# Attention's last tile and the start of the feed-forward part in a two-layer adaLN kernel: the tile reordered without its state sums, weight rounding on three engines, feed-forward's first group turned and rounded inside attention

## The chip, the cores and the metric

One core of one Trainium2 chip runs the whole computation in one launch. The metric is the device time of that launch in microseconds, as the median of several runs. The engines are TensorE (PE; its weight loads are PEld), VectorE (DVE), ScalarE (ACT), GpSimd (POOL) and SyncE (SP), which issues the transfers.

## The reference, cut to what matters

Two transformer layers over x of (2, 1024, 256), each an attention-like part and a feed-forward part, each behind a layer norm whose scale and shift come from a conditioning vector. Layer 0's attention is linear attention: 16 heads, 4 key/value heads, features elu(rope(q)) + 1, and a state that runs over the sequence. Its feed-forward part follows directly.

```python
h = _layernorm(x) * (1 + ca) + sa
# attention, per head, over the positions in order:
state = state + k_s[..., :, None] * v_s[..., None, :]
z = z + k_s
num = einsum('bhe,bhed->bhd', q_s, state)
den = einsum('bhe,bhe->bh', q_s, z)[..., None] + EPS
out = num / den
x = x + ga * (out @ Wo.T)
# feed-forward
h = _layernorm(x) * (1 + cb) + sb
h2 = silu(h @ w_gate) * (h @ w_up)
x = x + gb * (sparsify_2to4(h2) @ w_down)     # the two largest magnitudes of each four stay
```

Layer 1 (a test-time-training scan, then a mixture of experts) comes after that and is not touched but for where two of its buffers lie.

## The kernel before

The kernel is one program of four phases, each a block of its own with one instruction stream for each engine, ordered by hand with semaphores: attention_phase, ffn_phase, scan_phase, moe_phase. Between two blocks all engines meet. x stays in SBUF (x_sb) for the whole kernel, as 16 tiles of 128 positions, 8 for each of the two batches.

Attention walks the tiles as (c, b): c = 0 to 7 is the position in the sequence, b the batch, so the last two are (7, 0) and (7, 1). A tile is computed in chunks: within it the masked scores, before it the state. In step(c, b) TensorE turns the features of this tile (k, then four groups of q), computes for each of the four key/value heads the scores (L727), the numerators from masked scores and from the state (L735, L736), turns the normalised result (out_turn, L717), and at the end the sum k x v of this tile for the state (L774) and the output product with Wo (L786). Between these it projects q, k, v of the next tile (p(j), L689). VectorE masks the scores (masked, L575), normalises (L584, L587, L589), applies rope to the next tile's projections (L514, L517; GpSimd adds the two parts, L396), finishes the features (L529), adds the tile's sum to the state (L646), and adds the gated output to x (L658, L662). ScalarE drains what is turned (L419) and takes the exponentials. num is one PSUM buffer: numerators(g + 1) wait until normalise(g) has read numerators(g). score_masked and score have two slots.

Matrices that need more than fp32r's precision are split into a high part, rounded to fp32r, and a low part, the rest rounded: a product is three passes, high x high, low x high, high x low. For weights this is split_chunk, in chunks of 512 columns: chunk_high (L132 on VectorE, L130 on ScalarE) and chunk_low (L139). The four chunks of the feed-forward's gate and up weights go over the columns of the attention weights in w_hi and w_lo, so they can be written when the last projection, that of tile (7, 1) done during (7, 0), is through. Three of them are in the staging buffer a_stage early; the fourth reuses the first one's slot, and its transfer waits until the first has been rounded. In the last tile, which has no next tile to project, VectorE does all four splits between its masks and normalisations:

```python
for i in range(2 * FI // WCH):
    self.split_chunk(dve, NW + i, i * WCH)
    if i == 0:
        masked(1)
    if i == 1:
        normalise(1)
```

The feed-forward works on 4 groups of 4 tiles (512 positions). Of group 0 (tiles 0 to 3 of batch 0, long finished), VectorE takes the statistics (ffn_norms, L207, L210) and, after GpSimd's rstd (L214, L216), centres it into g_xn (ffn_centre, L223) at the end of the last attention tile. The rest of group 0 is in ffn_phase, behind the meeting of the engines: TensorE turns it (norm_turn, L1106), ScalarE applies scale and shift (drain_norm, L936), VectorE rounds it (split, L981, L983), and TensorE starts on hidden(0, 0), that is, gate and up product of 128 of the 1024 hidden columns, six matmuls of 512 columns each (L1117). m counts the 8 such blocks. In front of split(0) VectorE's queue has the statistics of group 1, behind it its centring; TensorE turns group 1 behind block m = 1.

## Time and profile before

| what | us |
|---|---|
| median of 3 runs | 1032.14 (1031.8 to 1033.04) |
| the profiled execution: time | 1031.37 |
| its span | 1029.6 |
| PE busy | 976.8 (95%) |
| DVE busy | 681.7 (66%) |
| ACT busy | 332.3 (32%) |
| POOL busy | 249.5 (24%) |
| mean granted clock of TensorE | 0.995 |

The profile is one execution. Times within it count from the start of its span. Attention takes the first 543 us, the feed-forward part of layer 0 follows. In a timeline each row is one instruction or a merged run of them: start, duration, engine, line of the kernel, operation, what it writes and reads, how often, and in brackets how long the engine was idle before it and what ended that. A duration includes the time an instruction spends in the pipeline, so the distance between starts tells what one costs its engine. The granted clock is 1.00 for 2.4 GHz and 0.50 for 1.2 GHz.

### The profile page before, as it was taken

Reading aid. Unit: us, or ns where it says so; the run is one execution under the profiler, and the core shown is the slowest. Engines: PE = TensorE matmul, PEld = TensorE weight load, DVE = VectorE, ACT = ScalarE, POOL = GpSimd, SP = SyncE. Lnnn points to the kernel's source line nnn. Section 1 sums busy time; section 2 is a strip of 40 time slices with the busy share of each in tenths; the row PEclk is TensorE's granted clock in tenths of the full one; section 3 lists DMA queues with packets and bytes.
Section 4 is the critical chain, followed back from the end, with each engine's and each line's share of the span. In section 5 each row is a group of like instructions: output and inputs, shape, how many; then the busy total and the mean of one; then the engine's idle time right before and its main releaser. Section 6 shows DMA issues by size and latency. Waiting matters only on the chain. (4 is left out here: it accounts for less than half of the span.)

```text
span 1029.6 us, 15693 instructions
## 1 busy us (share of the span) xinstructions
PE 976.8 (95%) x5994; PEld 791.1 (77%) x5994; DVE 681.7 (66%) x1494; ACT 332.3 (32%) x604; POOL 249.5 (24%) x320
## 2 busy tenths in 40 slices
PE   5899999999999999999978999998999999999997
PEld 4688888888888888888856788885666667778875
DVE  6766766666766667666565977765676776476556
ACT  4343333433333343334313323221122232422220
POOL 2232312222212323122201010023334554211011
PEclk9999999999999999999998999999999999999999
DMA  9400000000000000000004000002455340000000
GB/s 297 142 1 1 1 1 1 1 1 1 1 1 1 1 1 2 1 1 1 1 21 137 1 1 1 1 1 42 124 115 113 92 84 22 1 16 16 11 21 20
DMA packets 33051, 33.37 MB, mean 32 GB/s; under 512 B 6857, under 2 KB 26834, under 8 KB 32978
## 3 DMA queue, kind: packets, MB, share of 16 engines
q1 hardware_dynamic: 32978, 32.38, 11.9%
q8 instruction: 48, 0.79, 0.3%
q14 instruction: 25, 0.20, 0.1%
HBM read 23.98 MB, written 8.13 MB: 31 GB/s over the span
## 5 line engine op out<-in xcount | busy, mean ns | idle before, releaser
L396 POOL TENSOR_TENSOR rope_sum<-rope_cos,rope_sin 128x512 f32<-128x512 f32 x80 | 115.0, 1437 | 257.0 <-DVE rope_sin L517 257.0
L432 ACT ACTIVATE rope_exp<-rope_sum 128x512 f32<-128x512 f32 x80 | 50.5, 631 | 205.2 <-POOL rope_sum L396 205.1
L786 PE MATMUL proj<-wo_sb,attn_out_t 128*128 128x256 f32 x512 | 113.2, 379 | 0.7 <-issue 0.7
L786 PEld LDWEIGHTS proj<-wo_sb,attn_out_t 128*128 128x128 f32 x512 | 96.1, 190 | 13.4 <-issue 0.9
L735 PE MATMUL num<-v_ones,score_masked 128*128 128x129 f32 x512 | 99.2, 275 | 5.9 <-DVE score_masked L575 5.9
L736 PE MATMUL num<-state,q_t 128*128 128x129 f32 x512 | 99.0, 275 | 0.0
L2052 DVE SCALAR_TENSOR_TENSOR m_acc<-m_expert,gates,m_acc 128x256 f32<-128x256 f32 x128 | 61.9, 484 | 46.3 <-PE m_expert L2101 39.9
L735 PEld LDWEIGHTS num<-v_ones,score_masked 128*128 128x128 f32 x512 | 82.1, 191 | 13.4 <-DVE score_masked L575 8.0
L514 DVE TENSOR_TENSOR rope_cos<-proj,cos_sb 128x512 f32<-128x512 f32 x80 | 55.3, 691 | 52.3 <-PE proj L689 52.3
L689 PE MATMUL proj<-w_hi,a_h_hi 128*128 128x512 f32 x192 | 79.0, 493 | 4.1 <-DVE w_lo L139 2.4
L736 PEld LDWEIGHTS num<-state,q_t 128*128 128x128 f32 x512 | 77.7, 192 | 0.0
L529 DVE SCALAR_TENSOR_TENSOR feat<-rope_sum,rope_exp 128x512 f32<-128x512 f32 x80 | 69.1, 863 | 7.0 <-ACT rope_exp L434 7.0
L727 PE MATMUL score<-q_t,k_t 128*128 128x512 f32 x128 | 66.9, 605 | 0.0
L2101 PE MATMUL m_expert<-w_sb,m_act 128*128 128x256 f32 x256 | 62.9, 385 | 2.9 <-DVE m_acc L2052 2.9
L717 PEld LDWEIGHTS turn<-ident,feat 128*128 128x128 f32 x320 | 38.3, 143 | 32.3 <-issue 25.8
L1519 DVE TENSOR_TENSOR t_w<-g_ps,head_blocks 128x512 f32<-128x512 f32 x64 | 44.2, 691 | 27.9 <-PE g_ps L1727 27.9
L1128 PE MATMUL f_rows<-wd_sb,hidden 128*128 128x256 f32 x256 | 58.1, 380 | 3.3 <-DVE hidden L1021 1.5
L689 PE MATMUL proj<-w_lo,a_h_hi 128*128 128x512 f32 x192 | 60.9, 398 | 0.0
L689 PE MATMUL proj<-w_hi,a_h_lo 128*128 128x512 f32 x192 | 60.9, 398 | 0.0
L2101 PEld LDWEIGHTS m_expert<-w_sb,m_act 128*128 128x128 f32 x256 | 47.3, 190 | 14.5 <-DVE m_acc L2052 8.5
L1128 PEld LDWEIGHTS f_rows<-wd_sb,hidden 128*128 128x128 f32 x256 | 48.1, 190 | 11.8 <-issue 4.3
L717 PE MATMUL turn<-ident,feat 128*128 128x128 f32 x320 | 46.6, 277 | 9.8 <-ACT k_t L419 9.8
(250 smaller groups left out, 1883.6 us busy)
## 6 DMA issues: line engine op xcount, KB each, us to landing
kv_scratch<-t_kv SPq DMA_DIRECT2D x16, 256.0 KB, 2.4
kv_rows<-kv_scratch SPq DMA_DIRECT2D x32, 128.0 KB, 3.7
a_stage<-in_wqkv SPq DMA_DIRECT2D x6, 512.0 KB, 5.3
wo_sb<-in_wo SPq DMA_DIRECT2D x1, 2048.0 KB, 9.6
a_stage<-in_wgu SPq DMA_DIRECT2D x4, 512.0 KB, 9.7
out<-x_sb SPq DMA_DIRECT2D x16, 128.0 KB, 1.7
u_scratch<-u_rows SPq DMA_DIRECT2D x28, 64.0 KB, 2.9
t_u<-u_scratch SPq DMA_DIRECT2D x14, 128.0 KB, 2.2
```

The source lines that it names most:

```text
L396: pool.tensor_tensor(y[:, parity], t1[:, parity], t2[:, parity], ALU.add).then_inc(s["y_done"], 1)
L514: dve.tensor_tensor(t1[:, parity].rearrange("p (g d) -> p g d", d=HD // 2), proj[:, bank, :].rearrange("p (g d) -> p g d", d=HD // 2), cc. ...
L529: dve.scalar_tensor_tensor(dst, y[:, parity], 0.0, ex[:, parity], ALU.max, ALU.add).then_inc(s["feat_done"], 1)
L689: mm = pe.matmul(proj[:, bank, :], hh[:, parity, k, :], ww[:, k, cols], start=(i == 0 and k == 0), stop=(i == 2 and k == KD - 1))
L717: t = pe.transpose(turn[:, bank(j), r * P:(r + 1) * P], src[:, r * P:(r + 1) * P], ident[:])
L727: pe.matmul(score[:, g % 2, :], k_t[:, g, :], q_t[:, g, :], start=True, stop=True).then_inc(s["score_full"], 1)
L735: pe.matmul(dst, am[:, g % 2, r * P:(r + 1) * P], v[:, b, g, :], start=True, stop=False)
L736: mm = pe.matmul(dst, q_t[:, g, r * P:(r + 1) * P], state[:, b, g, :], start=False, stop=True)
L786: mm = pe.matmul(proj[:, b, 0:D], o_t[:, i, :], wo[:, i, :], start=(i == 0), stop=(i == H - 1))
L1128: mm = pe.matmul(rows[:, n % 2, 0:D], hid[:, g % 2, m, i * P:(i + 1) * P], wd[:, m, :], start=(m == 0), stop=(m == NM - 1))
L2052: ins = dve.scalar_tensor_tensor(acc[:, n % 2], expert[:, k % 2, j * D:(j + 1) * D], gates[:, g % 2, i, e:e + 1], acc[:, n % 2], ALU.mult, ...
L2101: mm = pe.matmul(expert[:, k % 2, j * D:(j + 1) * D], act_t[g % 2][:, e, toks], w2[:, e, :], start=True, stop=True)
```

## The change

Five edits, all around tile (7, 0), tile (7, 1) and the start of the feed-forward part:

- The state sums of the last two tiles (eight matmuls L774 and the addition L646 each) are left out; nothing reads them. The count of num_full and num_free is shifted by one for tile (7, 1) (num_item).
- The rounding of the four chunks is spread: chunks 0 and 1 wholly on VectorE at the end of tile (7, 0), in front of the dx multiplication; the high parts of chunks 2 and 3 on ScalarE (at the end of (7, 0), and in (7, 1) behind the q drains), their low parts on GpSimd behind its last rope addition, in front of ffn_rstd(0).
- Tile (7, 1) has an order of its own on TensorE and on VectorE: the scores run up to two groups ahead of the numerators, and VectorE has masks, normalisations, and group 0's statistics and centring between them.
- Group 0 of the feed-forward is turned by TensorE in tile (7, 1), into the score buffer, in front of out_turn(3); ScalarE drains it behind the last attn_out_t drain, VectorE rounds it behind normalise(3). ffn_phase begins without its norm_turn(0), drain_norm(0) and split(0).
- For that, f_h and the first slot of f_h_hi and f_h_lo share their place with the attention's modulation weights (a_wmod) and, later, with m_h and m_h_hi of the last phase (one_place).

The diff, cut to its core:

```diff
@@ run
+        block = [P, KD, GT * P]
+        self.wmod0, = self.one_place(("a_wmod", [P, KD, 6 * D], F32))
+        self.f_in = self.one_place(("f_h", block, F32), ("f_h_hi0", block, F32R), ("f_h_lo0", block, F32R))
+        self.e_h, self.e_h_hi = sb("m_h", block), sb("m_h_hi", [P, 2, KD, GT * P], F32R)
...
@@ attention, shared
+            def num_item(c, b, j):
+                return at(c, b, KVH + 1, j) - (1 if last(c, b) else 0)
...
@@ attention, GpSimd
                 walk(pool, step)
+                for i in (2, 3):
+                    self.chunk_low(pool, NW + i, i * WCH)
                 ffn_rstd(pool, 0)
...
@@ attention, ScalarE
+                    if last(c, b):
+                        self.chunk_high(act, NW + 3, 3 * WCH)
                     for g in range(KVH):
                         drain_turn(c, b, 5 + g, o_t[:, g * REP:(g + 1) * REP, :],
...
                     e(3)
                     e(4)
+                    if (c, b) == (NC - 1, 0):
+                        self.chunk_high(act, NW + 2, 2 * WCH)
+                    if last(c, b):
+                        for k in range(KD):
+                            act.wait_ge(f_s["turn_full"], k + 1)
+                            act.activation(f_h[:, k, :], score[:, k, :], ACT.Identity,
+                                           bias=mod_t[:, 0, SB_ * KD + k, 0:1],
+                                           scale=mod_t[:, 0, CB * KD + k, 0:1]).then_inc(f_s["h_done"], 1)
...
@@ attention, VectorE
                     if last(c, b):
-                        for i in range(2 * FI // WCH):
-                            self.split_chunk(dve, NW + i, i * WCH)
...
+                        masked(0)
+                        masked(1)
+                        normalise(0)
+                        masked(2)
+                        ffn_norms(dve, 0)
+                        normalise(1)
+                        masked(3)
+                        normalise(2)
+                        ffn_centre(dve, 0)
+                        normalise(3)
+                        dve.wait_ge(f_s["h_done"], KD)
+                        dve.tensor_copy(f_hi[:], f_h[:]).then_inc(f_s["hi_done"], 1)
+                        dve.wait_ge(f_s["hi_done"], 1)
+                        dve.tensor_tensor(f_lo[:], f_h[:], f_hi[:].bitcast(F32), ALU.subtract).then_inc(f_s["hl_done"], 1)
...
+                        if c < NC - 1:
+                            dve.wait_ge(s["num_full"], num_item(c, b, KVH) + 1)
...
+                        q_rope(4)
+                        f(3)
+                        if c == NC - 1:
+                            for i in range(2):
+                                self.split_chunk(dve, NW + i, i * WCH)
...
@@ attention, TensorE
+                    if last(c, b):
+                        scores(1)
+                        q_turn(3)
+                        numerators(0)
+                        scores(2)
+                        numerators(1)
+                        out_turn(0)
+                        scores(3)
+                        numerators(2)
+                        out_turn(1)
+                        numerators(3)
+                        out_turn(2)
+                        pe.wait_ge(f_s["xn_done"], GT)
+                        pe.wait_ge(s["score_free"], 2 + at(c, b, KVH, KVH))
+                        for k in range(KD):
+                            for i in range(GT):
+                                t = pe.transpose(score[:, k, i * P:(i + 1) * P], self.g_xn[:, i, k * P:(k + 1) * P], ident[:])
+                            t.then_inc(f_s["turn_full"], 1)
+                        out_turn(3)
...
+                        if c < NC - 1:
+                            pe.wait_ge(s["num_free"], num_item(c, b, KVH) + 1)
+                            for g in range(KVH):
+                                mm = pe.matmul(num[:, g // 2, (g % 2) * VW:(g % 2 + 1) * VW],
...
@@ feed-forward
-                drain_norm(0)
...
-                split(0)
...
-                norm_turn(0)
```

## Rows read from the trace of the kernel before

**Rows 1.** Busy time by stretch: length, busy time of each engine, granted clock, DMA.

```profile
520.00:540.00 20.00, 15.37 (x96) 12.65 (x96) 12.66 (x29) 2.39 (x4) 1.23 (x2) 1.00 0.08 25
```

**Rows 2.** Timeline of TensorE in the last tile, (7, 1).

```profile
509.69 1.04 PE L717 MATMUL turn<-ident,feat 128*128 128x128 f32 x8
...
511.53 1.06 PE L727 MATMUL score<-q_t,k_t 128*128 128x512 f32 x2
512.43 0.60 PE L717 MATMUL turn<-ident,feat 128*128 128x128 f32 x4
513.45 0.49 PE L735 MATMUL num<-v_ones,score_masked 128*128 128x129 f32 x2 [0.42 <-DVE score_masked L575]
...
515.34 1.02 PE L727 MATMUL score<-q_t,k_t 128*128 128x512 f32 x2
...
519.15 0.49 PE L735 MATMUL num<-v_ones,score_masked 128*128 128x129 f32 x2 [2.36 <-DVE score_masked L575]
...
521.04 0.60 PE L717 MATMUL turn<-ident,attn_out 128*128 128x128 f32 x4
521.48 1.02 PE L727 MATMUL score<-q_t,k_t 128*128 128x512 f32 x2
...
533.23 0.60 PE L717 MATMUL turn<-ident,attn_out 128*128 128x128 f32 x4
534.57 7.14 PE L786 MATMUL proj<-wo_sb,attn_out_t 128*128 128x256 f32 x32 [0.73 <-issue]
```

**Rows 3.** Timeline of VectorE in the last tile.

```profile
515.54 0.16 DVE L584 TENSOR_SCALAR den<-num 128x4 f32<-128x4 f32 x1 [2.15 <-PE num L736]
...
515.95 0.69 DVE L589 TENSOR_TENSOR attn_out<-num,rden 128x512 f32<-128x512 f32 x1
516.55 0.68 DVE L132 CAST w_hi<-a_stage 128x1024 fp32r<-128x1024 f32 x1
...
518.41 0.68 DVE L575 TENSOR_TENSOR score_masked<-score,causal 128x512 f32<-128x512 f32 x1
...
534.05 1.39 DVE L207 BATCH_NORM_STATS2 g_stats<-x_sb 128x6 f32<-128x256 f32 x4
...
537.14 1.38 DVE L223 TENSOR_SCALAR g_xn<-x_sb,g_mv,g_rstd 128x256 f32<-128x256 f32 x4 [1.42 <-POOL g_rstd L216]
```

**Rows 4.** Timeline of TensorE at the start of the feed-forward part.

```profile
542.96 1.07 PE L1106 MATMUL f_turn<-ident,g_xn 128*128 128x128 f32 x8 [1.25 <-PEq L272]
547.12 1.22 PE L1117 MATMUL gate_ps<-f_h_hi,w_hi 128*128 128x512 f32 x2 [3.09 <-DVE f_h_lo L983]
...
552.14 0.63 PE L1117 MATMUL gate_ps<-f_h_hi,w_hi 128*128 128x512 f32 x2
...
554.89 1.03 PE L1106 MATMUL f_turn<-ident,g_xn 128*128 128x128 f32 x8
```

**Rows 5.** Busy time by stretch, columns as in rows 1.

```profile
545.00:551.50 6.50, 4.38 (x10) 3.47 (x11) 3.25 (x6) 1.96 (x3) 3.27 (x9) 0.50 1.04 396
```

**Rows 6.** Timeline of all engines at the end of tile (7, 0).

```profile
500.04 1.05 PE L774 MATMUL num<-v_ones,feat 128*128 128x129 f32 x8
...
500.87 1.29 ACT L419 ACTIVATE attn_out_t<-turn 128x512 f32<-128x512 f32 x2
...
502.78 0.59 PE L786 MATMUL proj<-wo_sb,attn_out_t 128*128 128x256 f32 x2
```

**Rows 7.** The same timeline, a little later.

```profile
504.35 1.27 POOL L396 TENSOR_TENSOR rope_sum<-rope_cos,rope_sin 128x512 f32<-128x512 f32 x1 [1.09 <-DVE rope_sin L517]
504.62 1.55 DVE L529 SCALAR_TENSOR_TENSOR feat<-rope_sum,rope_exp 128x512 f32<-128x512 f32 x1 [0.35 <-ACT rope_exp L434]
```

**Rows 8.** Line L139 on GpSimd: duration in ns (min/median/max), first and last start, forms.

```profile
L139 POOL TENSOR_TENSOR w_lo<-m_act,w_hi x3: 1263/2374/2375, 812.0 to 846.5; 128x1024 fp32r<-128x1024 f32 x2, 128x512 fp32r<-128x512 f32 x1
```

**Rows 9.** Tile a_stage: ScalarE's casts, columns as in rows 8, and the transfers' time to landing.

```profile
L130 ACT ACTIVATE w_hi<-a_stage x5: 1042/1060/1063, 11.9 to 24.0; 128x1024 fp32r<-128x1024 f32 x5
...
DMA to landing us min/median/max: 3.8/5.8/11.0
```

More of the change, by code:

```diff
@@ L107, in run, with one_place @@
         self.moe_phase()
+    def one_place(self, *tensors):
+        with ExitStack() as ctx:
+            return [ctx.enter_context(self.nc.sbuf_tensor(n, shape, dt)) for n, shape, dt in tensors]
     def stage_for(self, ctx, name, first, slots):
@@ L739, in out_turn @@
                     def out_turn(g):
[L740 removed]
+                        pe.wait_ge(s["num_free"], 2 + num_item(c, b, g))
                         turn4(5 + g, on[:, g % 2, :])
@@ L752, in step @@
                     q_turn(2)
-                    if nxt:
-                        pe.wait_ge(s["hl_done"], at(c, b, 1, 2))
-                    p(0)
-                    numerators(0)
-                    scores(1)
-                    q_turn(3)
-                    p(1)
-                    numerators(1)
-                    out_turn(0)
-                    scores(2)
-                    p(2)
-                    numerators(2)
-                    out_turn(1)
-                    scores(3)
-                    p(3)
@@ L1116, in hidden @@
                             for k in range(KD):
-                                mm = pe.matmul(dst[:, n % 2, :], ww[:, k, cols], hh[:, g % 2, k, :],
+                                mm = pe.matmul(dst[:, n % 2, :], ww[:, k, cols], hh[g % 2][:, k, :],
                                                start=(i == 0 and k == 0), stop=(i == 2 and k == KD - 1))
```

111 lines of the change are left out of this document (52 added, 59 removed).

## The prediction, made before the changed kernel ran

> **What bounds the kernel now.** I read three views in this order. The page shows a kernel bound by TensorE, which is busy nearly all the time; among the busy times by stretch, 520 to 540 us stands out with PE busy for only 15.4 of 20 us, at a granted clock of 1.00 [rows 1]. The timeline of TensorE in that place shows the last attention tile, from its first turn at 509.69 to the output product that begins at 534.57, with holes of 2.4 us in front of a group's numerators (two such; 519.15 is the first) [rows 2]. VectorE's timeline names what fills the holes: between two masks it rounds a chunk of the feed-forward weights (cast and subtraction, 1.86 us from 516.55 to the mask at 518.41; four chunks, one after the other, stand among the masks), so masked(1), which needs nothing but a score and a free VectorE, is 3 us late [rows 3]. Then the phase changes: after the last x add TensorE turns group 0 (542.96), and waits for ScalarE and for two roundings on VectorE until 547.12 [rows 4]. During that wait the granted clock falls to 0.50, that is 1.2 GHz, and stays there to 551.5 [rows 5]. So from 509 to 552 us the end is set by a handover between engines, and from there by TensorE again.
>
> **The change, part by part.** All times are of the profiled execution: span 1029.6, time 1031.37, so 1.77 us lie outside; the median of the runs, 1032.14, is 0.77 above it. I follow the path in its times.
>
> (a) Tile (7, 0) loses the eight matmuls of the state sum, 0.89 us from 500.04 to the next group, and VectorE an addition. Not all of the 0.89 is gained: the output product also needs the last attn_out_t drain, which ScalarE ends at 500.87 + 1.29 = 502.16 whatever TensorE does. With 0.1 from a drain to the product (an estimate; a handover from TensorE to VectorE takes 0.20, 515.34 to 515.54 [rows 2, 3]) it starts at 502.26 instead of 502.78: 0.52 gained [rows 6]. The last tile's first turn moves from 509.69 to 509.17.
>
> (b) Two chunks move to VectorE at the end of (7, 0), after its last feature (504.62 + 1.55 = 506.17 before; about 505.4 now, since the projection ahead comes some 0.8 earlier) [rows 7]. They take 2 x 1.86 and a few hundredths, to 509.3. The dx multiplication waits for the end of the output product, 509.2 now, plus 0.2: no later than without the chunks by more than some hundredths, and TensorE does not wait for it in the next tile. Free. ScalarE rounds the third chunk from 508.1 (it waits for VectorE's second cast) to 509.2, at 1.06 us [rows 9], ahead of the k_t drain that is due at 509.8. Free.
>
> (c) GpSimd subtracts chunk three from 509.3. On GpSimd such a subtraction took 2.37 us (two rows of 128x1024) [rows 8], so to 511.7. In that time VectorE has an x add and the last feature, both of two SBUF operands. The trace shows what that means: a feature begun at 504.62 took 1.55 us beside a GpSimd addition that ran from 504.35 for 1.27 [rows 7]; operations of this size alone take 0.68, like the mask in rows 3. It stood still until 505.62. So I put x add at 511.7, feature at 512.1 and masked(0) at 512.7 to 513.4. The new order lets numerators(0) start at 513.7 only (below), so 0.25 us is left over: cost 0. Bounds: 0 (a gain is excluded, the operation is an added one) and +2.1 (the subtraction takes twice as long); I take 0 because two rows give its length.
>
> The Trainium skill, page "SBUF — State Buffer", section "Who interferes with whom", says that a VectorE instruction with two SBUF inputs and a GpSimd instruction that reads SBUF exclude each other for the whole instruction. The trace agrees for a 1.27 us operation; no row shows it for one of 2.37. By the rule the sum stays; without any exclusion it would also stay, as the slack covers it.
>
> (d) The tile's new order. From the first turn to scores(0) is 1.84 us (509.69 to 511.53). Then scores(0), q_turn(2), scores(1), q_turn(3) at 0.90 (511.53 to 512.43), 0.45 (four turns, 521.04 to 521.48), 0.90, 0.45 [rows 2]: numerators(0) start at 509.17 + 1.84 + 2.70 = 513.71. From there a cycle decides: numerators take 1.89 (513.45 to 515.34), VectorE answers 0.20 later, normalise takes 1.10 (515.54 to 515.95 + 0.69), and some 0.06 later, the remainder of my reckoning, the next numerators may start [rows 2, 3]: 3.25 us a group, in which the score (0.90) and a turn (0.45) fit. One group is late: the four statistics and aggregates (from 534.05 to 537.14 - 1.42 = 535.72, 1.67 us) [rows 3] stand behind masked(2) and push normalise(1) by 0.12. So numerators start at 513.71, 516.96, 520.33, 523.58. After the last: 1.89, out_turn(2) 0.45, the eight turns of group 0 0.89 give 526.81, where on(3) is just ready: out_turn(3) at 526.85. From it to the output product 1.34 us, as before (533.23 to 534.57) [rows 2]. The product starts at 528.2 instead of 534.57, 6.4 earlier. The state matmuls that this tile loses (eight again, 0.89 us) and the 2.4 us holes are in that.
>
> (e) What must not be late for this. Chunk four is loaded when chunk one is done (507.4) and landed 3.8 to 11.0 us after its issue [rows 9]; ScalarE rounds it behind the q_t drains, 514.5 to 515.6, GpSimd subtracts to 518.0, and only then takes rstd of group 0, whose statistics come at 519.1. The centring (1.4 us) stands between normalise(2), done at 523.5, and normalise(3) at 525.7, where VectorE is free [rows 3]. Behind ScalarE's wait for the chunk only out_turn drains are queued. The chain may end 4 us later before it costs. Free.
>
> (f) Group 0's drain and rounding, for which TensorE sat idle 3.1 us ahead of 547.12 [rows 4], now lie beside the output product of 7.1 us [rows 2]. Cover: they start with the last drain, at 528.1, and would have to take over 8 us to show. So behind the phase change TensorE can begin with gate matmuls where it turned before. That removes 542.96 to 547.12, 4.16 us [rows 4]. VectorE is free for norms and centring of group 1: 1.67, 1.42 for rstd and 1.38, so done 4.5 us into the phase [rows 3], and norm_turn(1) stands behind two hidden blocks, 5.5 us in (twice the 2.75 of (g)). Free, with 1 us.
>
> (g) The clock. Before, the 12 gate and up pairs of groups m = 0 and 1 took 5.02 us (547.12 to 552.14, mostly at 0.50) and 2.75 (552.14 to 554.89, at full clock) [rows 4, 5]. If TensorE's only hole at the change of phase is the 1.3 us between product and first matmul, I take the full clock, since holes of 2.4 us in the tile left it at 1.00 [rows 1, 2]: 2.27 gained. Bounds: 0 (clock falls all the same) and 2.3.
>
> Sum: 6.4 (with 0.52 in it) + 4.16 + 2.27 = 12.8. Everything later hangs on TensorE and moves along unchanged. 1031.37 - 12.8 = 1018.6 for such an execution, span 1016.8; with 0.77, a median of 1019.3.
>
> **Rivals.**
> R1, the clock falls anyway. For it: the drain before the product and the barrier now stand 7 us apart, two holes near one another, and a long transfer starts there. Against it: before, the same two holes stood there, and the eight turns behind them took 1.07 us, no more than the eight at 509.69 with 1.04 [rows 2, 4]; the fall came in the wait of 3.1 us behind them. It costs 2.3: 1021.6.
> R2, the three-engine rounding comes back as a wait: GpSimd's subtraction holds x add and feature, or the rounding of chunk four is late for rstd. The first costs whatever exceeds 511.95, the second begins when the chunk's chain ends after 522.2, 4 us later than I put it. A chain 2 to 3 us worse than my figures gives 1021 to 1022.
> R3, the other side: chunk four's transfer. It is issued late and everything hangs on it in one line: ScalarE's cast, GpSimd's subtraction, rstd, centring, normalise(3), the product. Each us of landing beyond some 11 us after the issue delays the end by one. To be slower than before by 2 it must land 26 us after its issue, against 11.0 at most [rows 9]: 1034.5 (1019.3 + 15.2).
> R4, the holes close but the gain is not passed on: VectorE, the busiest engine after TensorE in the feed-forward part, becomes the limit of group 0. Its first product then moves less than TensorE. Against it: the page has TensorE busy nearly all the time there, so it does not wait for VectorE. I put the loss at no more than the 3 us of VectorE's norms and centring of group 1: 1022.3.
>
> **How the numbers follow.** The forecast has 0.66, R1 0.12, R2 0.11, R4 0.04, R3 0.02; 0.05 is left for a larger gain (a shorter phase change, as less is waiting in it: down to 1016.5). The forecast's own range is 1018 to 1020.5. To hold 8 in 10 I go to 1017.3 below and 1022.2 above. A measurement can tell about 0.2%, 2 us, from no change. Faster 0.96, same 0.02, slower 0.02.
>
> **What would show it.** Right: numerators of the last tile 3.2 to 3.4 us apart, an output product beginning near 528, no f_turn group before the first gate matmul at 536.5, granted clock 1.00 there and 2.75 us for m = 0. GpSimd's two w_lo rows at about 2.4 us, ending before 519. Wrong: a hole in front of q_turn(3) or numerators(0) released by VectorE, g_rstd late behind w_lo, a stretch at 0.50 after the barrier, or new waits of TensorE on hidden or silu_gate in group 0.

## The result and the profile after

The changed kernel took 1021.43 us (median of 13 runs, 1018.61 to 1032.28), the kernel before 1033.66 in as many runs beside it (1031.41 to 1035.42): a ratio of 0.9891, interval [0.9871, 0.9911], 12.2 us faster. The forecast was 1019.3 with a range of 1017.3 to 1022.2. The profiled execution took 1021.04 with a span of 1019.1; before it was 1031.37 and 1029.6.

| us | before | after |
|---|---|---|
| median of 13 runs each | 1033.66 | 1021.43 |
| span of the profiled execution | 1029.6 | 1019.1 |
| PE busy | 976.8 (95%) | 978.2 (96%) |
| DVE busy | 681.7 (66%) | 676.8 (66%) |
| ACT busy | 332.3 (32%) | 334.1 (33%) |
| POOL busy | 249.5 (24%) | 254.6 (25%) |
| second q turn of the kernel, the first with a long wait | 36.60 | 38.75 |
| output product of (7, 0) | 502.78 | 504.44 |
| output product of (7, 1) | 534.57 | 530.36 |
| first gate matmul | 547.12 | 538.75 |
| after the feed-forward part: next modulation vectors | 683.11 | 673.22 |
| first gradient of the scan | 710.99 | 701.09 |
| first expert product | 893.6 | 882.95 |

The stretch that opened the argument, busy time of each engine, granted clock and DMA, columns as in [rows 1]:

```profile
520.00:540.00 20.00, 17.17 (x107) 14.47 (x106) 10.28 (x29) 5.01 (x7) 1.30 (x3) 1.00 0.01 3
```

TensorE's timeline of the last tile and of the start of the feed-forward part, which answers to [rows 2, 4] (start, duration, instruction, idle before it and what ended that):

```profile
511.43 1.04 PE L744 MATMUL turn<-ident,feat 128*128 128x128 f32 x8
...
513.27 1.06 PE L754 MATMUL score<-q_t,k_t 128*128 128x512 f32 x2
...
515.90 0.39 PE L762 MATMUL num<-v_ones,score_masked 128*128 128x129 f32 x2
...
519.13 0.46 PE L762 MATMUL num<-v_ones,score_masked 128*128 128x129 f32 x2 [0.42 <-DVE attn_out L616]
...
522.44 0.46 PE L762 MATMUL num<-v_ones,score_masked 128*128 128x129 f32 x2
...
525.75 0.46 PE L762 MATMUL num<-v_ones,score_masked 128*128 128x129 f32 x2 [0.85 <-DVE attn_out L616]
...
528.05 1.04 PE L796 MATMUL score<-ident,g_xn 128*128 128x128 f32 x8
528.97 0.66 PE L744 MATMUL turn<-ident,attn_out 128*128 128x128 f32 x4
530.36 7.14 PE L832 MATMUL proj<-wo_sb,attn_out_t 128*128 128x256 f32 x32 [0.73 <-issue]
538.75 0.70 PE L1162 MATMUL gate_ps<-f_h_hi,w_hi 128*128 128x512 f32 x2 [1.25 <-PEq L281]
...
541.62 0.63 PE L1162 MATMUL gate_ps<-f_h_hi,w_hi 128*128 128x512 f32 x2
...
544.42 1.03 PE L1151 MATMUL f_turn<-ident,g_xn 128*128 128x128 f32 x8
```

The numerators follow each other every 3.23 to 3.31 us, where one step took 5.70 before (513.45 to 519.15). The holes of 2.4 us are gone; 0.42 and 0.85, both ended by a normalisation, are left. No turn stands between the meeting of the engines and the first gate matmul. Two blocks of m take 5.67 us (538.75 to 544.42) instead of 7.77, and the stretch that answers to [rows 5] stands at full clock:

```profile
538.70:545.00 6.30, 6.25 (x30) 5.15 (x31) 4.18 (x14) 3.12 (x4) 2.98 (x10) 1.00 0.79 281
```

GpSimd's timeline, its two subtractions:

```profile
511.42 2.36 POOL L148 TENSOR_TENSOR w_lo<-a_stage,w_hi 128x1024 fp32r<-128x1024 f32 x1 [4.29 <-ACT w_hi L139]
517.72 2.35 POOL L148 TENSOR_TENSOR w_lo<-a_stage,w_hi 128x1024 fp32r<-128x1024 f32 x1 [3.94 <-ACT w_hi L139]
```

VectorE's timeline, what it does beside the first of them, and group 0's rounding, which now lies beside the output product:

```profile
512.09 1.98 DVE L689 TENSOR_TENSOR x_sb<-x_sb,a_dx 128x256 f32<-128x256 f32 x1
513.99 0.68 DVE L556 SCALAR_TENSOR_TENSOR feat<-rope_sum,rope_exp 128x512 f32<-128x512 f32 x1
514.59 0.68 DVE L602 TENSOR_TENSOR score_masked<-score,causal 128x512 f32<-128x512 f32 x1
...
531.63 0.69 DVE L648 CAST f_h_hi<-f_h 128x1024 fp32r<-128x1024 f32 x1 [2.72 <-ACT f_h L496]
532.36 1.23 DVE L650 TENSOR_TENSOR f_h_lo<-f_h,f_h_hi 128x1024 fp32r<-128x1024 f32 x1
```

**Where the 10.5 us of the two spans come from**, as differences of the table's steps: the start of the kernel +2.15; from there to the product of (7, 0) -0.49; to the product of (7, 1) -5.87; to the first gate matmul -4.16; to the modulation vectors -1.52; to the scan's first gradient -0.01; the scan -0.75; the rest +0.15. The first step ends in the second q turn. The +2.15 lies 460 us ahead of the first edit, in a place whose instructions are the same. It is the spread of single executions, and the granted clock goes with it: between 26 and 28 us it was 1.00 in the profile of before and 0.50 in the one after (the last part of the next section shows the rows).

### The profile page after: what moved, and what is told of

It is laid out like the page before. It is cut to its first block and busy times, and to the rows that moved or that the text cites. A ratio compares the mean times of both kernels' runs of the same rounds, so it can differ in the third digit from the quotient of the medians.

```text
span 1019.1 us, 15660 instructions
## 1 busy us (share of the span) xinstructions
PE 978.2 (96%) x5978; PEld 790.9 (78%) x5978; DVE 676.8 (66%) x1488; ACT 334.1 (33%) x606; POOL 254.6 (25%) x322
## 5 line engine op out<-in xcount | busy, mean ns | idle before, releaser
L832 PEld LDWEIGHTS proj<-wo_sb,attn_out_t 128*128 128x128 f32 x512 | 96.0, 190 | 13.7 <-issue 1.3
```

The lines of the kernel that those rows point to most:

```text
L832: mm = pe.matmul(proj[:, b, 0:D], o_t[:, i, :], wo[:, i, :], start=(i == 0), stop=(i == H - 1))
```

## The experiments

All medians are of runs on the same chip as a kernel before; "product" is the output product of (7, 1), "gate" the first gate matmul, "mod" the modulation vectors behind the feed-forward part. The steps from one to the next are read in the profiles.

**e1 and e12: the changed kernel again**, with no edit, beside two groups of the others.

> The changed kernel once more. Theory A (the handover gained what the steps say, 12.8 us, and the rest of the distance is chance at the start of the kernel): the output product of the last tile begins 25.9 us behind the one of tile (7, 0) (504.44 to 530.36 in the first profile), the first gate matmul 8.4 us later, and where the first tile's first turn stands (36.6 before, 38.75 in the first profile) changes from run to run in both kernels; ratio 0.988. Theory B (the change itself makes the start slower): the first turn stands at 38.7 again and the kernel before has it at 36.6 each time; ratio 0.990.

> The changed kernel a third time, for the spread of its runs: 4 of 19 runs so far stood above 1025. Theory T (the change brings the far runs): some of six above 1025 again, more often than the kernel before stands 4 us above its median (3 of 47). Rival (they come to both kernels): none, or as many in both.

1020.48 (1019.04 to 1030.57, 6 runs; ratio 0.9884 [0.9846, 0.9921]) and 1021.62 (1019.51 to 1032.41, 6 runs; 0.9892 [0.985, 0.9934]). In each, five runs agree within 2.2 us and one lies 10 higher; such runs are called far runs from here on. In e1's profile the product came 25.91 us behind that of (7, 0) and the gate 8.40 later, as theory A has it; the second q turn stood at 38.73, which theory B expects too, and only e2 and e14 below part the two.

**e2: group 0's turn, drain and rounding back behind the meeting of the engines.**

```diff
@@ attention, TensorE, tile (7, 1)
-                        for k in range(KD):
-                            for i in range(GT):
-                                t = pe.transpose(score[:, k, i * P:(i + 1) * P], ...)
...
@@ feed-forward
+                drain_norm(0)
...
+                split(0)
...
+                norm_turn(0)
```

> The changed kernel with group 0's turn, drain and rounding back in the feed-forward phase; all else stays changed. Theory A: against the changed kernel 4.16 us for the serial steps come back and 2.27 for the clock, and the last tile is 0.9 shorter by the eight turns: together 5.5 us slower than it, with a stretch at 0.50 behind the wait. Rival (the clock term is wrong, it falls only by chance): 3.3 us slower, the granted clock in the first hidden blocks at 1.00.

1026.83 (1025.31 to 1032.88, 12 runs; 0.9945 [0.9927, 0.9963]), 6.35 above e1. TensorE's timeline, and the busy time by stretch:

```profile
536.65 1.06 PE L1137 MATMUL f_turn<-ident,g_xn 128*128 128x128 f32 x8 [1.25 <-PEq L281]
540.81 1.22 PE L1148 MATMUL gate_ps<-f_h_hi,w_hi 128*128 128x512 f32 x2 [3.09 <-DVE f_h_lo L1014]
```

```profile
539.00:545.80 6.80, 4.99 (x12) 3.93 (x13) 3.05 (x6) 1.66 (x2) 2.96 (x9) 0.51 1.03 390
```

The wait of 3.09 us is back, and with it the fall of the clock: product to gate takes 12.55 us again instead of 8.39, gate to mod 136.81 instead of 134.47. That is 4.16 + 2.34 = 6.50. I had deducted 0.9 for the turns, which the last tile no longer issues, and that was wrong: product to product did not get shorter (25.91 against 25.92), since the turns lie in TensorE's wait for normalise(3). So, against this changed kernel, (f) and (g) are worth all of what they were put at, and the turns inside the tile cost nothing.

**e3 and e9: e2 with the wait filled**, by 28 and by 20 turns of the identity into a PSUM buffer that is not in use. Only the activity of TensorE in the wait differs from e2.

```diff
                 norm_turn(0)
+                for i in range(28):        # 20 in e9
+                    pe.transpose(rows[:, i % 2, 0:P], ident[:], ident[:])
```

> As the one before, with 28 more turns of the identity on TensorE in the wait between group 0's turn and the first gate matmul (their result is not used). Theory A (idle time in front lowers the clock): no stretch at 0.50, blocks m = 0 and 1 take 5.5 us together, 2.2 us faster than without the filling. Rival (the clock falls for another cause, the transfers that start there): the stretch at 0.50 stays and the time is that of the one before, or up to 0.3 more.

> The kernel with group 0 turned in the feed-forward phase again and 20 instead of 28 turns filled in. The one with 28 had the clock stretch gone as expected (2.3 us shorter to the modulation vectors) and still lost 10 us against the one without filling, in stretches at 0.50 in the scan, 230 us later. Theory F (keeping the clock up there makes the scan lose it, for whatever cause): again 1030 us or more in most runs, mean clock below 0.990. Rival (an accident of where the phases fall in those runs): 1024.5 in most runs, 2.0 us faster than without filling.

In the place itself both agree with the reading of (g): gate to mod took 134.51 and 134.53 us, 2.3 less than in e2, at a granted clock of 1.00. The medians do not follow: 1036.34 (1030.82 to 1047.43, 12 runs; 1.0022 [0.9999, 1.0045]) and 1027.04 (11 of the 12 between 1025.03 and 1035.47, the twelfth 1403.28 at a mean clock of 0.654; 0.9938 [0.9918, 0.9959]). e3's profile is its second slowest run, 1046.76. The profile of e3 shows where its time went, in the scan, which took 202.65 us from its first gradient to the first expert product where the changed kernel took 181.86. Its timelines there, VectorE's row and then TensorE's, and two stretches, the filled wait and one in the scan:

```profile
770.24 0.29 DVE L1545 TENSOR_TENSOR u_rows<-kv_rows,z_ps 128x128 f32<-128x128 f32 x1 [2.64 <-DMA kv_rows<-kv_scratch]
```

```profile
770.58 0.50 PE L1758 MATMUL g_ps<-u_rows,kv_rows 16*128 16x128 f32 x8 [1.84 <-DVE u_rows L1545]
...
814.79 0.50 PE L1758 MATMUL g_ps<-u_rows,kv_rows 16*128 16x128 f32 x8 [1.69 <-DVE u_rows L1545]
...
859.00 0.50 PE L1758 MATMUL g_ps<-u_rows,kv_rows 16*128 16x128 f32 x8 [2.05 <-DVE u_rows L1545]
```

```profile
539.00:545.80 6.80, 6.77 (x47) 5.95 (x45) 4.49 (x14) 3.33 (x4) 3.47 (x10) 1.00 0.94 332
820.00:830.00 10.00, 10.00 (x59) 5.63 (x62) 3.94 (x10) 0.77 (x2) 2.83 (x4) 0.50 0.27 78
```

TensorE waits 1.84 us for u_rows, which need the kv_rows that a transfer brings, from 772.1 the granted clock is 0.50, and at half the clock TensorE is busy all the time and slow. The same follows the waits of 1.69 and 2.05 (from 816.4 and 860.8). None of this is near the edit. Neither expectation fits e9: it has not e3's loss in most of its runs, and not the gain of 2.0 either. The reading of (g) is shown in its place. No gain of the whole is measured, but e2's and e9's intervals (0.9927 to 0.9963 and 0.9918 to 0.9959) are too wide to exclude 2 us. Why the scan of e3 was disturbed in its profile, and why e3's median is long, is not shown.

**e4: the first subtraction on GpSimd made twice**, the first time into columns of w_lo that chunk four overwrites later.

```diff
+                pool.tensor_tensor(w_lo[:, :, 3 * WCH:4 * WCH], self.raw(NW + 2, WCH),
+                                   w_hi[:, :, 2 * WCH:3 * WCH].bitcast(F32), ALU.subtract).then_inc(self.w_ready2, 1)
                 for i in (2, 3):
                     self.chunk_low(pool, NW + i, i * WCH)
```

> The changed kernel with GpSimd's subtraction of chunk three done twice (the first time into the columns of chunk four, which are written again later). Theory A (x add and the last feature stand still as long as GpSimd works): the x add of tile (7, 0) takes 4.3 us, masked(0) starts 2.4 later, 0.25 of it is slack, 2.1 us slower. Rival (VectorE gets in between two GpSimd operations, or the operations are not held): at most 0.5 us slower.

1023.88 (1023.15 to 1028.94, 6 runs; 0.9911 [0.9885, 0.9937]). Product to product took 27.59 us instead of 25.91, 1.7 more. Its timelines, GpSimd's second subtraction (the first ran from 511.00 to 513.36), VectorE's next two operations, and TensorE's wait:

```profile
513.44 2.43 POOL L149 TENSOR_TENSOR w_lo<-a_stage,w_hi 128x1024 fp32r<-128x1024 f32 x1
```

```profile
511.69 1.96 DVE L694 TENSOR_TENSOR x_sb<-x_sb,a_dx 128x256 f32<-128x256 f32 x1
513.57 2.85 DVE L561 SCALAR_TENSOR_TENSOR feat<-rope_sum,rope_exp 128x512 f32<-128x512 f32 x1
```

```profile
516.48 0.66 PE L749 MATMUL turn<-ident,feat 128*128 128x128 f32 x4 [1.25 <-DVE feat L561]
```

VectorE did get in between the two GpSimd instructions, for one operation: x add was held by the first (1.96 us, where the same operation takes 0.43 in e10), the feature by the second (2.85 instead of 0.68). So x add finishes at about the time it did anyhow, and the price is 1.7, not the bound of 2.1. That a single subtraction costs nothing is read in the changed kernel itself: its numerators(0) follow q_turn(3) at 515.90 with no idle time in front, 0.6 us after masked(0) has ended.

**e10: the opposite of it, all four chunks on VectorE** at the end of tile (7, 0), the parts on ScalarE and GpSimd gone.

```diff
-                for i in (2, 3):
-                    self.chunk_low(pool, NW + i, i * WCH)
...
-                            for i in range(2):
+                            for i in range(4):
                                 self.split_chunk(dve, NW + i, i * WCH)
```

> The changed kernel with all four chunks on VectorE at the end of tile (7, 0), none on ScalarE and GpSimd. Theory A: chunk four lands some 4.5 us after its issue, VectorE is through 4.7 us later than with two chunks, the x add no longer stands still (1.6 us back), numerators(0) start 2.2 us later: 2.2 us slower than the changed kernel. Rival (the spread is worth nothing): 0.

1026.86 (1021.78 to 1030.7, 6 runs; 0.9915 [0.9886, 0.9944]). Product to product took 27.45 us, 1.5 more than in the changed kernel; I had expected 2.2. VectorE's rounding ends at 515.07, x add follows at once, and TensorE waits once (VectorE's timeline, then TensorE's):

```profile
513.92 1.22 DVE L148 TENSOR_TENSOR w_lo<-a_stage,w_hi 128x1024 fp32r<-128x1024 f32 x1
515.07 0.42 DVE L679 TENSOR_TENSOR a_dx<-proj,gate_b 128x256 f32<-128x256 f32 x1
515.52 0.43 DVE L683 TENSOR_TENSOR x_sb<-x_sb,a_dx 128x256 f32<-128x256 f32 x1
```

```profile
516.60 0.66 PE L738 MATMUL turn<-ident,feat 128*128 128x128 f32 x4 [1.11 <-DVE feat L550]
```

The use of ScalarE and GpSimd is thus worth 1.5 us of the 5.87. The other 4.3 are the rounding gone from between the masks and normalisations of (7, 1), the new order, and the state sum left out; no run takes these three apart. The remainder of this kernel's loss in its profile is in the scan (189.1 us instead of 181.86), behind a wait of 1.66 us for u_rows, and 1.27 us in front of it (29.14 instead of 27.87 from mod to the first gradient).

**e7: the state sum back in tile (7, 0).**

```diff
-                return at(c, b, KVH + 1, j) - (1 if last(c, b) else 0)
+                return at(c, b, KVH + 1, j)
...
-                        if c < NC - 1:
+                        if True:
```

> The changed kernel with the state sum of tile (7, 0) put back (of no use to the result); tile (7, 1) stays without. Theory A (the drain of attn_out_t hides a part): the output product of (7, 0) starts 0.52 us later against the tile's first turn than in the changed kernel, and with VectorE's addition in front of its chunks the first mask of (7, 1) 0.6 later; 0.5 to 0.6 us slower. Rival (all of the matmuls' time counts): 0.9 us slower. Rival (nothing of it counts): 0.

1021.86 (1019.96 to 1024.36, 4 runs; 0.987 [0.9826, 0.9914]); no median tells 0.8 us, so the place decides. In e7 the product of (7, 0) begins 4.59 us behind out_turn(2), exactly as before the change; without the sum it is 3.84. ScalarE's drain in the kernel with the sum and in the changed one:

```profile
502.98 1.29 ACT L436 ACTIVATE attn_out_t<-turn 128x512 f32<-128x512 f32 x2
```

```profile
503.28 1.07 ACT L436 ACTIVATE attn_out_t<-turn 128x512 f32<-128x512 f32 x2
```

The gain is 0.75, not 0.52: the row of before, 1.29 for the two drains, had a pause between them that the sum itself made. Without it they follow closely and take 1.07. The eight matmuls took 0.89; the other 0.14 is TensorE's wait for the end of the second drain (504.35, the product at 504.44). VectorE's addition, which was to delay the first mask, cost nothing: product to product took 25.84 us.

**e5 and e6: where f_h lies.** TensorE's pairs of fp32r matmuls of 512 columns (a row with x2) start 0.466 us apart in the first and third group of the feed-forward part of the changed kernel and 0.455 in the second and fourth, where the kernel before has 0.455 or less in all four. In the changed kernel f_h, f_h_hi0 and f_h_lo0 start 32 bytes off from their place within 64 bytes in the kernel before. e6 shifts them by one pad of 32 bytes; e5 has this and a second pad, behind the buffers, which puts the other slot back as well.

```diff
+        self.pad0 = sb("pad0", [P, 8])
         self.wmod0, = self.one_place(("a_wmod", [P, KD, 6 * D], F32))
...
+        self.pad1 = sb("pad1", [P, 8])        # e5 only
```

> The changed kernel with 32 bytes of padding in front of the shared place of f_h, f_h_hi0 and f_h_lo0, and 32 more behind it, so that these start where the buffers of the kernel before started within 64 bytes. Theory P (the new place of the first slot slows the matmuls that read it: 0.466 us for a pair of 512 columns in groups 0 and 2 against 0.452 in 1 and 3): all four groups at 0.452, from the first gate matmul to the modulation vectors 133.7 instead of 134.5 us, 0.75 us faster in all. Rival (the difference is one of the group or of the time, not of the place): 134.5 as before, no change.

> As the one before, but with the first padding only, which moves the first slot to a multiple of 64 bytes and the second slot (f_h_hi1, f_h_lo1) off it. Theory P: groups 0 and 2 at 0.452, groups 1 and 3 at 0.466. Rival: 0.466 stays with groups 0 and 2.

Changed kernel, group 0 and then group 1:

```profile
558.36 0.63 PE L1162 MATMUL up_ps<-f_h_hi,w_lo 128*128 128x512 f32 x2
558.83 0.63 PE L1162 MATMUL up_ps<-f_h_lo,w_hi 128*128 128x512 f32 x2
...
564.82 0.61 PE L1162 MATMUL gate_ps<-f_h_hi,w_hi 128*128 128x512 f32 x2
565.27 0.62 PE L1162 MATMUL gate_ps<-f_h_hi,w_lo 128*128 128x512 f32 x2
```

e6, group 0 and then group 1:

```profile
558.11 0.62 PE L1163 MATMUL gate_ps<-f_h_lo,w_hi 128*128 128x512 f32 x2
558.57 0.61 PE L1163 MATMUL up_ps<-f_h_hi,w_hi 128*128 128x512 f32 x2
...
564.13 0.63 PE L1163 MATMUL up_ps<-f_h_hi,w_hi 128*128 128x512 f32 x2
564.60 0.63 PE L1163 MATMUL up_ps<-f_h_hi,w_lo 128*128 128x512 f32 x2
```

With the one pad the slots change roles: groups 0 and 2 at 0.454 on the mean, groups 1 and 3 at 0.466. With both, groups 0 and 2 are at 0.455 and groups 1 and 3 at 0.458, so the second slot is not quite as quick as before. Gate to mod is 134.47 us in the changed kernel, 134.26 in e6 and 134.00 in e5, so 0.48 of the feed-forward part's loss is the place of a buffer, where 0.75 was expected. Other profiles repeat it: 134.46 to 134.53 in the eight others without a pad and without the fall of the clock, 133.94 to 134.03 in the three others with both pads (e8, e11, e15). e5's median is 1020.23 (1018.95 to 1020.96, 6 runs; 0.9854 [0.9823, 0.9886]), e6's single run 1018.88. e5 is the fastest version measured in several runs, but no median separates it from the changed kernel.

**e8 and e11: is the late start curable?** In e8 the gate products of the conditioning vector stand behind the last projection of the start instead of before it, so that the last projection and what hangs on it start earlier (e5's pads are in). e11 adds turns of the identity ahead of the start's last projections and before the second q turn, to keep TensorE active.

```diff
-                    if j == 4:
-                        pe.wait_ge(s["wide_done"], 1)
-                        pe_gates(pe)
+                pe.wait_ge(s["wide_done"], 1)
+                pe_gates(pe)
...
+                    if j >= 2:                                       # e11 only
+                        for i in range(5):
+                            pe.transpose(score[:, 1, 0:P], ident[:], ident[:])
...
+                    if isinstance(c, int) and c == 0 and b == 0:     # e11 only
+                        for i in range(10):
+                            pe.transpose(score[:, 1, 0:P], ident[:], ident[:])
```

> The padded kernel with one thing more, at the kernel's start: the gate products of the modulation, 16 matmuls that stood between the last two projections, come behind the last. It tests where the profiles differ, at the start: TensorE is idle there for 5.0 us (33.7 to 38.75) for a chain that begins with the last projection at 31.1, while that one's weights were ready at 28.6. Theory S (the chain projection, rope, exponential, k_t drain sets the first turn): first turn near 36.3 instead of 38.7, 2.0 to 2.4 us faster than the padded kernel. Rival (the gate products and their reading on ScalarE come on the path in its place): within 0.5 us of the padded kernel.

> The padded kernel with the gate products behind the last projection, and with turns of the identity filled into TensorE's waits at the start (5 before each projection from the third on, 10 before the second q turn; results not used). Without filling that order gained 3.5 us up to the first turn (35.15 instead of 38.65) and not a microsecond in the median, while TensorE ran at 0.50 from 25.1 to 31.9. Theory C (the clock at the start takes the gain): no stretch at 0.50 in the first 45 us, 1018 or less. Rival (filled turns delay the projections as much as the clock gives): 1020.

The second q turn begins at 37.62 in e8 and 35.53 in e11, against 38.65 in e5, and the product of (7, 0) 1.45 and 3.52 us earlier than in e5 (502.62 and 500.55 for 504.07). (The 35.15 in the expectation above is the row of the very first turns, which e5 has at 32.58, so the order alone gained 1.0 us up to the second q turn and not 3.5.) e11 had no stretch at 0.50 in its first 45 us, as theory C wants it, e8 one from 25 to 32. The medians show neither gain: 1020.27 (1018.08 to 1020.89, 6 runs; 0.9854 [0.9822, 0.9886]) and 1023.99 (1019.68 to 1031.16, 10 runs; 0.9915 [0.9888, 0.9942]). In e8's profile the clock is at 0.50 once more at 673.7, in e11's at 671.9, and from mod to the scan's first gradient both took 29.1 us instead of e5's 27.88; e11's clock fell again at 835.7 in the scan, just ahead of a gradient that had waited 1.64 us. In these two profiles what is won at the start was lost in later places.

**e13, e14, e15: work in the scan's waits.** The profiles of e3, e9, e10 and e11 have long scans (202.65, 192.06, 189.1 and 187.8 us, against some 182). In them TensorE waited six times for 1.64 to 2.05 us for u_rows, three times in e3 and once in each of the others, and a stretch at 0.50 goes with each. In the ten profiles whose scan stayed at full clock (before, after, e1, e2, e4 to e8 and e12) no such wait was over 1.22 us; there it was 1.01 in the kernel before and 0.74 in the changed one. The three kernels have six small matmuls before each tile's first gradient, from the second tile on: e13 is the changed kernel with them, e14 the kernel before with them, e15 is e8 with them.

```diff
+                            if n == 0 and c:
+                                idle_u(6)
                             gradient(c, n)
```

> The changed kernel with six small matmuls of no effect (they add to unused columns, as the kernel's own idle_u does) ahead of each scan tile's first gradient, where TensorE waits up to 1.8 us for the transfer of kv_rows and behind which the scan's stretches at 0.50 began in three profiles (769.9, 769.7 and 772.1). Theory W (this wait is where the far runs lose their clock): no run above 1024, median 1021 or less, scan 181.6 to 182.9 us in the profile. Rival (the clock falls there for another cause, or the six delay the gradient): far runs stay, or the median is 0.5 to 3 us higher.

> The kernel before with the same six matmuls. Theory W: its far runs (4 of 70 at 1039 and more) go too; median 1033. It says whether the far runs are the scan's own, in both kernels, or of the change: if the change brings them, this kernel shows nothing new.

> Padding, gate products behind the last projection, and the six matmuls together: what would be the fastest version. Theory W: 1018 to 1020.3 with no run above 1023. Rival (each gives back to the clock what it gains): 1020.3 and more, as the padded kernel.

1030.15 (1027.87 to 1031.03, 11 runs; 0.9942 [0.9918, 0.9967]), 1040.73 (1039.76 to 1042.52, 11 runs; 1.0046 [1.0023, 1.007]) and 1026.25 (1025.62 to 1027.77, 6 runs; 0.9909 [0.988, 0.9938]). The matmuls cost more than they save: e13's scan took 190.95 us, 9.1 more, at full clock throughout, so the medians that theory W expected (1021 or less, 1033, and 1018 to 1020.3) were all missed by 6 to 9 us. But none of the 28 runs lies far out: each kernel's spread is 3.2 us or less, against 13.7 in the 13 runs of the changed kernel, and 7 of the 21 runs of the kernel before beside them were above 1038. This speaks for theory W's cause and does not prove it, since e5, e6 and e8 had no far run either, in 13 runs without the six matmuls. And the change is worth 1040.73 - 1030.15 = 10.6 with them in both.

The rows show that the wait comes from when SyncE issues the transfer, not from how long the transfer takes. From issue to landing a transfer of kv_rows took at most 5.1 us in e3's profile and 5.2 in the changed kernel's; it was issued later against the scan's work. The two rows, e3 and then the changed kernel:

```profile
765.81 0.78 SPq L1311 DMA_DIRECT2D kv_rows<-kv_scratch  x2
```

```profile
759.60 0.78 SPq L1322 DMA_DIRECT2D kv_rows<-kv_scratch  x2
```

VectorE's preceding step of u_rows began at 765.89 and 760.76: the issue was 0.08 us ahead of it in e3 and 1.16 ahead in the changed kernel, and the next u_rows followed the issue by 4.43 and 4.41. At all six long waits the issue was only 0.04 to 0.22 us ahead of that step; at thirteen waits of 0.42 to 1.22 us, in nine profiles, it was 0.51 to 1.84 ahead.

e14's profile settles the start as well. Its edit is in the scan, the start is that of the kernel before, and the second q turn stands where it stands in the changed kernel:

```profile
38.74 1.00 PE L717 MATMUL turn<-ident,feat 128*128 128x128 f32 x4 [5.04 <-ACT k_t L419]
```

The other way round, e2, a changed kernel at its start, has it at 36.48. So the 2.15 us are no part of the change. The clock goes with them. The stretch from 26 to 28 us in before, e2, the changed kernel and e14:

```profile
26.00:28.00 2.00, 2.00 (x11) 1.72 (x11) 2.00 (x2) 0.55 (x1) 1.42 (x1) 1.00 1.10 348
26.00:28.00 2.00, 2.00 (x11) 1.77 (x10) 2.00 (x2) 0.64 (x2) 1.29 (x1) 1.00 1.10 348
26.00:28.00 2.00, 2.00 (x6) 1.54 (x6) 2.00 (x2) 0.42 (x1) 1.54 (x1) 0.50 1.09 346
26.00:28.00 2.00, 2.00 (x6) 1.54 (x6) 2.00 (x2) 0.39 (x1) 1.58 (x1) 0.50 1.10 348
```

Of the 14 profiles whose start is not edited, 12 have such a stretch between 24 and 30 us and their second q turn at 38.5 to 38.8; the kernel before and e2 have none and are the two early ones.

e14's profile shows one thing more, in the last tile, which its edit does not touch. The second hole of 2.4 us between two groups, in the kernel before and in e14, and e14's clock behind it:

```profile
524.86 0.49 PE L735 MATMUL num<-v_ones,score_masked 128*128 128x129 f32 x2 [2.35 <-DVE score_masked L575]
```

```profile
527.06 0.80 PE L735 MATMUL num<-v_ones,score_masked 128*128 128x129 f32 x2 [2.36 <-DVE score_masked L575]
```

```profile
527.00:530.00 3.00, 2.94 (x13) 2.94 (x14) 1.83 (x3) 0.00 (x0) 0.00 (x0) 0.50 0.00 0
```

The same hole left the clock at 1.00 in one execution and took it to 0.50 in the other, from 526.9 to 530.3. Product to product took 33.36 us there instead of 31.79. So what the change removes is worth 5.87 us against one profile of the kernel before and 7.44 against the other.

## Why the prediction came out as it did

The measured median lies inside the range, 2.1 us above the point: the mechanism was right, some sizes were not. Step by step, in the profiles, before against after:

(a) The product of (7, 0) begins 0.75 us earlier behind out_turn(2), forecast 0.52. The mis-sized term is the drain, put at 1.29 as in [rows 6]: it held a pause of the removed sum and measured 1.07. e7 puts all 0.75 back. From the second q turn to this product the two profiles differ by only 0.49, since single executions differ by some tenths in the 460 us in front (460.4 to 462.1 us from the second q turn to out_turn(2), in the 14 profiles with the same start).

(b) Right. ScalarE's cast of the third chunk stood at 510.28, which is the forecast 508.1 moved by the 2.18 of this execution's later product (504.44 for 502.26).

(c) Right, cost 0. The subtraction took 2.36 us (put at 2.37), x add stood still until it ended and took 1.98, the feature followed at 513.99. The rule cited there, in the page "SBUF — State Buffer" of the Trainium skill, section "Who interferes with whom", that the two exclude each other for the whole instruction, held in this trace for 2.36 us; in e4 it held for each of two instructions in a row, with one VectorE operation let in between.

(d) Right. The numerators were forecast 3.25 to 3.37 apart and were 3.23, 3.31 and 3.31; from product to product the kernel gained 5.87 us, the forecast's 6.4 less 0.52 being 5.88. e10 shows how it is made up: 1.5 from ScalarE and GpSimd, 4.3 from the rest. That these 5.87 count against a tile without a fall of the clock was luck of the profile: in e14 the same tile of the kernel before was 1.57 longer.

(e) Right: ScalarE's cast of chunk four followed the last q drain at 516.60 without a wait for the transfer, its subtraction ended at 520.07, rstd was ready at 522.56, normalise(3) waited only for its numerators.

(f) Right to 0.01: 4.16.

(g) The cause was right, the size was not: 2.27 forecast, 1.52 measured. The two blocks won 2.10 us and the rest of the feed-forward part took 0.58 more. Of the 0.75 that are missing e5 finds 0.48 in the place of f_h, which the prediction did not look at although the diff moves it: the forecast read one_place as a matter of space alone. The other 0.27 stay unexplained; in e5 the pairs of groups 1 and 3 were still at 0.458. Nor was the 5.02 for the first block a fixed price. In e14, with the same wait of 3.09 us in front, it took 4.42, and gate to mod 135.40 instead of 135.99. The reason given, that holes of 2.4 us left the clock at 1.00, does not hold in every execution, as e14 shows. The clock stayed up behind the phase change all the same: no profile of a kernel that turns group 0 inside attention has a stretch at 0.50 there.

Terms (a), (d), (f) and (g) sum to 12.3 us where 12.8 was forecast. The medians of all runs agree with this as far as their spread allows (the interval of the 12.2 above is 2 us either way): 25 runs of the changed kernel (with e1 and e12) give 1021.33, 91 runs of the kernel before 1033.82, a difference of 12.5.

**What failed is the base of the sum, "with 0.77, a median of 1019.3", and with it the sentence "Everything later hangs on TensorE and moves along unchanged"; in the sum itself the term (g), 2.27 forecast and 1.52 measured.** The 0.77 from the profile to the median came from three runs. In the 13 runs beside the changed kernel the median was 1033.66, so 2.29 above the profiled 1031.37, and over all 91 runs it was 1033.82. The profile from which the forecast started was a quick one: it had full clock from 26 to 28 us and a start some 2 us shorter than in 12 of 14 profiles, full clock in the last tile, where e14 lost 1.57, and no fall in the scan. Places that the edit does not touch do not simply move along: the start has 2.1 us of spread, the step from mod to the first gradient took 27.9 us or 29.1 with more of it at 0.50 (e3, e7, e8, e10 and e11), and the scan took 6 us and more longer in four profiles. So of the 2.1 us between point and median 1.5 are the base (1033.66 - 1032.14) and 0.6 the difference (12.8 - 12.2). The terms give 0.5 for the latter, 0.75 lost in (g) less 0.23 more in (a), but medians with an interval of 2 us can't confirm it.

Rival R1, the clock falling anyway, would have given 1021.6, nearly the measured median, and is wrong all the same: the granted clock of the stretch was 1.00. R2 stayed out (no hole ahead of q_turn(3) released by VectorE; 1.25 us in e4 and 1.11 in e10). R4 stayed out too: behind the second block TensorE waited 1.30 us in all up to the modulation vectors, 1.65 before. R3 needed a transfer that did not come late.

**Open.** The changed kernel had 5 runs of 25 above 1025, the kernel before 11 of 91 above 1038. Whether the change makes them more frequent can't be told from such counts. Left without them, the medians are 1020.58 and 1033.35, 12.8 apart. The far runs are runs with a lower clock in both kernels: the five had a mean granted clock of 0.983 to 0.990 and the other twenty 0.993 to 0.997, the kernel before's eleven 0.981 to 0.987 and its others, where the clock is on record, 0.990 and more. That the clock falls in the scan in them is read from four profiles (e3, e9, e10, e11) and from the 28 runs of e13 to e15, and not from a profile of a far run of the changed kernel itself. What makes SyncE issue kv_rows later in one execution than in another was not tried. Nor is it settled why e3, whose edit ends 230 us before the scan's wait, fell into it so often.

## What to carry to other kernels

Price a change by the steps between fixed points of the trace, and hold each against the same step of the changed kernel: here two terms came out within 0.01 us and two within 0.23 and 0.75, while the total wandered by 2 us with places that nobody had touched. Read the granted clock of the steps in front first: a single profile can be a quick one, and three runs put the median 1.7 us below that of 91. Before a drain or a rounding is priced by its row, see whether the row holds a pause that the removed work itself made. A buffer that only moves is a part of the change: compare its start within 64 bytes with where it was, for every operand that TensorE streams.

## What the runs showed of the hardware

- Pairs of fp32r matmuls of 512 columns started 0.466 us apart with the moving operand at one place in SBUF and 0.454 with it 32 bytes further, and the difference went with the buffer from one group to the other (e5, e6).
- The granted clock fell to 0.50 at all six waits of 1.64 to 2.05 us in the scan, and at none of up to 1.22 in ten other profiles. In the last attention tile of before, holes of 2.36 us left it at 1.00 [rows 1, 2]; in e14 the same instructions, with the second hole again 2.36 us, ran at 0.50 from 526.9 to 530.3. So the length of a wait alone does not decide.
- In 12 of 14 profiles with the same start TensorE ran at 0.50 for 3 to 4 us between 24 and 30 us, in 2 it did not, and these reached the second q turn 2.1 us earlier.
- Between two GpSimd instructions of 2.36 and 2.43 us, back to back, VectorE was let in for a single operation with two SBUF operands (e4).
- Filling a wait of TensorE brought the clock back in its place (2.3 us in e3 and e9) and gave no measured gain in the medians (1036.34 and 1027.04 against e2's 1026.83).
